# Expert slots of an attention and mixture-of-experts block: hidden transposes behind half of the next up projection, copies in halves, weight splits behind the gating

## What is computed

```
x = x + tanh(g_xattn) * xattn(layernorm(x), ctx)        # 16 heads of 64
xf = layernorm(layernorm(x)) * gamma + beta             # 2048 x 256
probs = softmax(xf @ router_w.T)                        # 8 experts
gate = the two largest probabilities of each token
for each expert e:
    xe = xf * gate[:, e]
    g, u = split(xe @ gate_up_w[e].T)                   # 512 and 512 wide
    out += (silu(g) * u) @ down_w[e].T                  # back to 256
x = x + tanh(g_ffn) * (x' + out)                        # x' is the normed input of this part
```

## Time and profile before

| | us |
|---|---|
| median of three runs (544.29 to 546.94) | 546.45 |
| the profiled execution | 547.43 |
| its span, first to last instruction | 545.1 |
| TensorE busy in the span | 511.6 |
| VectorE busy | 340.2 |
| ACT busy | 290.6 |
| POOL busy | 213.3 |

### The profile page before, as it was taken

The page is one execution under the profiler, slowest core; times in us unless marked ns, Lnnn a source line. Parts: engine busy times, 40 slices in busy tenths (PEclk is TensorE's granted clock), DMA queues, the critical chain, the costliest instruction groups (busy, mean ns, idle before and its releaser), DMA issues.

```text
span 545.1 us, 11962 instructions
## 1 busy us (share of the span) xinstructions
PE 511.6 (94%) x3712; PEld 475.5 (87%) x3712; DVE 340.2 (62%) x811; ACT 290.6 (53%) x881; POOL 213.3 (39%) x242
## 2 busy tenths in 40 slices
PE   7899999999999999999999798989889999999992
PEld 6698999999999999999998687877778888888881
DVE  5956676667768778587685777578745563333330
ACT  3446666656555556456655565576346654444341
POOL 5063100305604569318374168335423343332332
PEclk9999999999999999999998989999999999999997
DMA  8700000499991011100023066554386653343421
GB/s 232 239 0 2 1 1 2 140 304 297 288 290 62 0 39 38 39 0 10 31 78 99 0 207 190 123 134 116 79 240 167 138 78 46 54 60 58 59 30 20
DMA packets 50418, 54.35 MB, mean 100 GB/s; under 512 B 8832, under 2 KB 46464, under 8 KB 50368
## 3 DMA queue, kind: packets, MB, share of 16 engines
q1 hardware_dynamic: 43216, 44.38, 28.5%
q0 software_dynamic: 7152, 9.33, 10.8%
HBM read 24.12 MB, written 29.58 MB: 99 GB/s over the span
## 4 chain that ended last, share of the span: by engine, by line
PE 67%; DVE 12%; issue 6%; DMA 4%; ACT 3%; DVEq 2%; POOLq 2%; POOL 2%; SPq 1%; ACTq 0%
PE bank L914 13%; PE bank L739 9%; PE bank L685 8%; PE bank L763 8%; PE bank L701 8%; PE bank L934 6%; PE bank L715 5%; DMA out_dram<-yq,tok 2%; PE bank L748 2%; PE bank L924 2%; PE bank L859 2%; PE bank L659 1%; DVE nmax L1213 1%; PE bank L782 1%; DVEq L1171 1%
## 5 line engine op out<-in xcount | busy, mean ns | idle before, releaser
L1022 ACT ACTIVATE probs<-bank,nmax 128x154 f32<-128x154 f32 x256 | 98.3, 395 | 81.6 <-DVE nmax L1213 81.6
L602 POOL DMA_INDIRECT out_dram<-yq,tok x39 | 60.8, 1560 | 119.2 <-ACT yq L1101 57.9
L739 PE MATMUL bank<-vdiag,pT 128*128 128x128 f32 (+2 forms) x640 | 79.8, 272 | 1.0 <-DVE oT_lo L1237 0.6
L739 PEld LDWEIGHTS bank<-vdiag,pT 128*128 128x128 f32 (+1 forms) x640 | 77.6, 194 | 1.7 <-DVE oT_lo L1237 1.1
L1213 DVE TENSOR_REDUCE nmax<-bank 128x2 f32<-128x308 f32 x128 | 57.0, 476 | 34.1 <-PE bank L701 33.9
L914 PE MATMUL bank<-gu_hi,xqT_hi 128*128 (+1 forms) x156 | 67.9, 435 | 0.0
L914 PE MATMUL bank<-gu_lo,xqT_hi 128*128 (+1 forms) x156 | 61.5, 394 | 0.0
L914 PE MATMUL bank<-gu_hi,xqT_lo 128*128 (+1 forms) x156 | 61.3, 393 | 0.0
L1580 DVE TENSOR_TENSOR hidT_lo<-bank,hidT_hi 128x512 fp32r<-128x512 f32 x39 | 26.9, 690 | 47.0 <-ACT hidT_hi L1094 46.7
L1575 DVE TENSOR_TENSOR hid<-hid,bank 128x512 f32<-128x512 f32 x39 | 26.8, 687 | 43.1 <-PE bank L914 42.9
L1022 ACT ACTIVATION_READ_ACCUMULATOR probs<-bank,nmax 128x1 f32 x256 | 53.2, 208 | 0.0
(11 more groups left out here) (211 smaller groups left out, 1323.6 us busy)
## 6 DMA issues: line engine op xcount, KB each, us to landing
expert_queue<-zrow SPq DMA_DIRECT2D x8, 2184.5 KB, 23.0
gu_raw<-in_gate_up_wT_dram SPq DMA_DIRECT2D x16, 512.0 KB, 4.3
xq<-expert_queue SPq DMA_DIRECT2D x39, 128.0 KB, 2.9
dn_raw<-in_down_wT_dram SPq DMA_DIRECT2D x8, 512.0 KB, 4.3
x<-in_x_dram SPq DMA_DIRECT2D x4, 512.0 KB, 13.2
out_dram<-out SPq DMA_DIRECT2D x8, 256.0 KB, 4.6
wq_raw<-in_L_xattn_Wq_dram SPq DMA_DIRECT2D x1, 1024.0 KB, 11.7
wo_raw<-in_L_xattn_Wo_dram SPq DMA_DIRECT2D x1, 1024.0 KB, 10.4
```

The source lines that it names most:

```text
L602: nc.gpsimd.indirect_dma_start(out[:, :], bass.IndirectOffsetOnAxis(tok[j % (2 * RT)][:, 0:1], 0), yq[p][:, :], None, compute_op=ALU.add). ...
L739: last = nc.tensor.matmul(at[:, col0 + j0 * DH:col0 + j0 * DH + n], pT[u % 2][0:rows, b, :], v, start=(b == 0), stop=(b == NBLK - 1), skip ...
L1022: last = nc.scalar.activation(probs[u % 4][:, j * NKB:(j + 1) * NKB], S_BANK[hf][:, m * NKB:(m + 1) * NKB], ACT.Exp, bias=nmax[:, u % 4, j ...
```

## The change

The diff is given whole, without blank lines. On TensorE the hidden transposes of tile j-1 go behind the first up half of tile j, so that they stand next to the row transposes of tile j+1. They write two banks: the first two chunks HT_BANK, the last two the bank in which tile j-2's result lay (hidden_bank; TA for the first and the last tile), and so a wait on e_ysb, that this result was read, stands between them. ACT and VectorE copy the hidden rows in two halves, and down waits for each half apart. On VectorE rows_T comes ahead of gated, and the splits that LOWS names come behind gated; two splits, in EARLY_LOWS, stay ahead of both.

```diff
@@ -100,8 +100,9 @@
     HIGHS = {2: ((2, 0), (2, 1)), 3: ((2, 2),), 4: ((3, 0), (3, 1)), 5: ((3, 2),), 6: ((4, 0),), 7: ((4, 1),), 8: ((4, 2),),
              12: ((5, 0),), 13: ((5, 1),), 14: ((5, 2),), 15: ((6, 0),), 16: ((6, 1),), 17: ((6, 2),), 18: ((7, 0),), 19: ((7, 1),), 20: ((7, 2),)}
-    LOWS = {3: ((2, 0),), 4: ((2, 1), (2, 2)), 5: ((3, 0),), 6: ((3, 1),), 7: ((3, 2), (4, 0)), 8: ((4, 1),), 9: ((4, 2),),
-            13: ((5, 0),), 14: ((5, 1),), 15: ((5, 2),), 16: ((6, 0),), 17: ((6, 1),), 18: ((6, 2),), 19: ((7, 0),), 20: ((7, 1),), 21: ((7, 2),)}
+    LOWS = {2: ((2, 0),), 3: ((2, 1),), 4: ((3, 0),), 5: ((3, 1),), 6: ((4, 0),), 7: ((4, 1),), 8: ((4, 2),),
+            12: ((5, 0),), 13: ((5, 1),), 14: ((5, 2),), 15: ((6, 0),), 16: ((6, 1),), 17: ((6, 2),), 18: ((7, 0),), 19: ((7, 1),), 20: ((7, 2),)}
+    EARLY_LOWS = {4: ((2, 2),), 6: ((3, 2),)}
     ON_POOL = ((0, 2), (1, 0), (1, 1), (1, 2))
     with ExitStack() as ctx:
@@ -160,6 +161,10 @@
             hidT_lo = fsb("hidT_lo", [P, KF, P], F32R)
             yq = [fsb(f"yq{n}", [P, D]) for n in range(RT)]
         G_BANK, U_BANK, XT_BANK, HT_BANK, Y_BANK = bank[0], bank[1], bank[6], bank[4], (bank[5], bank[7])
+
+        def hidden_bank(j, h):
+
+            return HT_BANK if h == 0 else TA if j in (0, MT - 1) else Y_BANK[(j + 1) % 2]
         def expert_at(sp, rank):
@@ -919,17 +924,21 @@
                 def transpose_hidden(i, p):
                     j = RT * i + p
                     pe.wait_ge(s["e_hid"], j + 1)
-                    at_least(pe, s["e_hT_lo"], j)
+                    at_least(pe, s["e_hT_lo"], 2 * j)
                     for c in range(KF):
-                        last = nc.tensor.transpose(HT_BANK[:, c * P:(c + 1) * P], hid[:, c * P:(c + 1) * P], ident[:, :])
+                        if c == 2 and 0 < j < MT - 1:
+                            at_least(pe, s["e_ysb"], j)
+                        last = nc.tensor.transpose(hidden_bank(j, c // 2)[:, c % 2 * P:(c % 2 + 1) * P],
+                                                   hid[:, c * P:(c + 1) * P], ident[:, :])
                     last.then_inc(s["e_hT_ps"], 1)
                 def down(i, p, rank):
                     j = RT * i + p
-                    pe.wait_ge(s["e_hT_lo"], j + 1)
                     at_least(pe, s["e_ysb"], j - 1)
                     n = 0
                     for c in range(KF):
+                        if c % 2 == 0:
+                            pe.wait_ge(s["e_hT_lo"], 2 * j + c // 2 + 1)
                         for h, part in ((hidT_hi, dn_hi), (hidT_lo, dn_hi), (hidT_hi, dn_lo)):
                             last = nc.tensor.matmul(Y_BANK[p % 2][:, 0:D], h[:, c, :], weights(part, rank, c * D, D),
                                                     start=(n == 0), stop=(n == 3 * KF - 1))
@@ -947,12 +956,10 @@
                         pe.wait_ge(s["table"], 1)
                     rank = rank_of(i, p)
                     tile_before = (i - 1, RT - 1) if p == 0 else (i, p - 1)
+                    up(i, p, rank, 0, G_BANK, "e_gate", "e_silu")
+                    if j in (2, 3):
+                        turn_features(NI, j - 2)
                     transpose_hidden(*tile_before)
-                    if j == 3:
-                        turn_features(NI, 1)
-                    up(i, p, rank, 0, G_BANK, "e_gate", "e_silu")
-                    if j == 2:
-                        turn_features(NI, 0)
                     if j == 3:
                         router_logits(NI, 0, TA)
                         router_logits(NI, 1, TA)
@@ -1091,7 +1098,10 @@
                     j = RT * i + p
                     act.wait_ge(s["e_hT_ps"], j + 1)
                     at_least(act, s["e_y"], j)
-                    nc.scalar.copy(hidT_hi[:, :, :].rearrange("p c t -> p (c t)"), HT_BANK[:, :]).then_inc(s["e_hT_hi"], 1)
+                    for h in range(2):
+                        part = slice(2 * h, 2 * h + 2)
+                        nc.scalar.copy(hidT_hi[:, part, :].rearrange("p c t -> p (c t)"),
+                                       hidden_bank(j, h)[:, 0:2 * P]).then_inc(s["e_hT_hi"], 1)
                 def scaled(i, p):
@@ -1576,14 +1586,16 @@
                 def hidden_T(i, p):
                     j = RT * i + p
-                    dve.wait_ge(s["e_hT_hi"], j + 1)
-                    nc.vector.tensor_tensor(hidT_lo[:, :, :].rearrange("p c t -> p (c t)"), HT_BANK[:, :],
-                                            hidT_hi[:, :, :].rearrange("p c t -> p (c t)").bitcast(F32), ALU.subtract).then_inc(s["e_hT_lo"], 1)
+                    for h in range(2):
+                        part = slice(2 * h, 2 * h + 2)
+                        dve.wait_ge(s["e_hT_hi"], 2 * j + h + 1)
+                        nc.vector.tensor_tensor(hidT_lo[:, part, :].rearrange("p c t -> p (c t)"), hidden_bank(j, h)[:, 0:2 * P],
+                                                hidT_hi[:, part, :].rearrange("p c t -> p (c t)").bitcast(F32), ALU.subtract).then_inc(s["e_hT_lo"], 1)
                 def expert_slot(i, p, more=True):
                     j = RT * i + p
                     hidden_T(*((i - 1, RT - 1) if p == 0 else (i, p - 1)))
-                    for part in LOWS.get(j, ()):
+                    for part in EARLY_LOWS.get(j, ()):
                         split_low(dve, *part)
                     if j == 2:
                         second_norm(1)
@@ -1593,9 +1605,11 @@
                     if j == COUNT_SLOT:
                         count_rows(NI)
                         number_rows(NI)
-                    gated(i, p)
                     if more:
                         rows_T(i + (p + 1) // RT, (p + 1) % RT)
+                    gated(i, p)
+                    for part in LOWS.get(j, ()):
+                        split_low(dve, *part)
                     if j == COUNT_SLOT - 2:
                         router_probs(NI)
                         choose(NI, 0)
```

## The result

The changed kernel took 552.01 us (median of 7 runs, 550.02 to 553.21) against 546.94 for the kernel before (7 runs, 544.29 to 548.08). The ratio is 1.0107, with a 95% interval of 1.0086 to 1.0128: 4.7 to 7.0 us slower, about 5.9; the two medians differ by 5.1. The profiled execution took 552.01 us, span 549.3. The forecast was 549.0 with a range of 544.0 to 554.5: slower, as the larger chance said, and inside the range, but about 3 us short, and outside the forecast's own range (547.5 to 550.3).

A forecast was written before the change was run, and what follows sets the result against it. TensorE's own work was taken to bound the steady slots (0 us), late VectorE to hold the early ones; routing terms summed to +2.53, say +2.55, on 547.43, less 0.98 to the median: 549.0 us, range 544.0 to 554.5.

The forecast's parts named there:

- Steady slots, 26 x 0: The 26 late expert slots, bound by TensorE's own work at 4.86 us each: nothing saved or lost, 0 us.
- TensorE's queue: Look-up before the up half: margin 0.04 to 0.14 us; rival without that margin, +1.3 to +7.3 us, chance 0.23.
- T: Start of a slot's hidden transposes; down was due at T + 2.04, the next up half at T + 3.48.
- Transposes next to each other: Steady slots: six transposes standing together cost 0.11 us each as before, so nothing is saved.
- (a): Slot 3: the logits wait 1.1 us for the copy of xfT where they waited 0.37, +0.75 us.
- (b): Slot 4: the new wait for e_ysb inside the transposes, with ACT's yq late, delays the hidden copy, +0.45 us.
- (c): VectorE, tile 3 to tile 8: halves +0.30, gaps that do not close +0.75, first half releasing down -0.27 us.
- (d): After each late down the expert look-up is bare, 0.28 us with an up half behind it: +0.15 us.
- (e): Slot 12: the output starts later as slot 10's gating is behind its rows, and tile rows queue behind it: +0.40 us.
- (f): Early splits in slots 4 and 6, counted in (c); tail: last scatter-add waits for the one before, 0 us.
- The clock: Rival: slot 9's wait passes 2 us and the granted clock falls, +1.7 to +3.4 us, 550.7 to 552.4, chance 0.07.
- Faster: Rival: splits behind the gating close VectorE's gaps and slot 3's waits go, 543.3 us, chance 0.13.

The follow-up runs named there:

- before_pool: The kernel before with two weight splits, (3, 0) and (3, 2), made by POOL instead of VectorE: 547.88 us, ratio 1.0050.
- lookup_ahead: The kernel after with the look-up of the next tile's expert moved in front of the second up half: 550.06 us, ratio 1.0071.
- lookup_twice: The kernel after with the expert look-up before the first up half made twice for tiles 14 to 38: 567.85 us, ratio 1.0402.
- whole_copies: The kernel after with hidden copies whole and from one bank for tiles 13 to 38: 566.52 us, ratio 1.0363.
- tile3_whole: The kernel after with tile 3 transposed into one bank and copied whole, without the wait for yq: 552.57 us in one profile.
- splits_alone: The kernel before with only the new split tables and their place behind the gating and the rows: 548.24 us, ratio 1.0044.
- features_first: The kernel after with ACT's copy of xfT in slot 3 moved ahead of the hidden copies: 551.26 us, ratio 1.0077.
- all_edits: The kernel after with look-up moved ahead, xfT copied first, tile 3 whole and two splits on POOL: 550.25 us, ratio 1.0089.

## Why the prediction was right in the sign and short in the size

**Steady slots, 26 x 0: the step that failed.** Three margins were named, and the thinnest, TensorE's queue with 0.04 to 0.14 us, was not there. The first half of the hidden copies was released at T + 1.46 as worked out (T = 483.57; VectorE's pair begins at 484.61 and one half takes 0.42: 485.03). The up half's first weights were due at T + 3.37 (0.12 after 486.82) and forecast for T + 3.34; they loaded at T + 3.45 (487.02). The chain had been put together from a measured 1.78 us and an estimated 0.1 for a second wait; it was 0.1 longer, and 0.1 a slot is 2.5 us. That is the mean: down was released at T + 1.46 in every steady slot, but from tile 12 to 22 a slot lost 0.14 and later 0.07; what makes the queue slower in the earlier ones was not told apart. The mechanism stood among the rivals at 1.3 to 7.3 us, with chance 0.23: its lower part is what happened. Its reason was the wrong one, though. It was tied to long loads (649 ns), but here the look-up is as short as before:

```profile
L905 PEldq TENSOR_LOAD <-table x55: 283/287/422, 400.6 to 535.7; - x55
```

The reason given against that rival held: 2 of these 55 loads took over 320 ns, where before 17 of 54 did. That the long ones come only with an SP issue beside them was a little too strong: in the trace of before 15 of the 17 have one.

The figure of about 600 ns (the Trainium skill, "DMA: Bandwidth & Descriptors", section "Latency and other measured facts") would have given 555.0 by the prediction's estimate; the trace disagrees on the load (287 ns), and the time came out at 552.0. The chain fails already with a short load, because everything between release and next up half goes through one queue. A margin that is a small difference of large terms should not have been booked as zero.

**Transposes next to each other: nothing.** Right: with the look-up moved, the slot is 4.89 us.

**(a) Slot 3, +0.75.** The wait for xfT came, 0.92 us after 0.37, a little under the 1.1 forecast, and tile 2's down stands 0.61 behind; taking the cause away gave back 1.1 us. Right.

**(b) Slot 4, +0.45.** The wait for yq came (0.32), and from tile 2 to tile 3 the change lost 0.61. Removing it gave 0.34 to 0.57. Right.

**(c) VectorE, +0.78.** From tile 3 to tile 8 the loss was 1.06. VectorE waited 0.56 and 0.89 us for rows in slots 4 and 7 (forecast 0.6 and 1.0) and 0.66 and 0.61 for hidden copies behind slots 5 and 6 (0.6 and 0.4), 2.72 in all, where 2.7 was forecast:

```profile
357.73 0.42 DVE L1578 TENSOR_TENSOR xqT_lo<-bank,xqT_hi 128x256 fp32r<-128x256 f32 x1 [0.56 <-ACT xqT_hi L1089]
367.96 0.76 DVE L1592 TENSOR_TENSOR hidT_lo<-bank,hidT_hi 128x256 fp32r<-128x256 f32 x2 [0.66 <-ACT hidT_hi L1103]
374.12 0.76 DVE L1592 TENSOR_TENSOR hidT_lo<-bank,hidT_hi 128x256 fp32r<-128x256 f32 x2 [0.61 <-ACT hidT_hi L1103]
375.77 0.42 DVE L1578 TENSOR_TENSOR xqT_lo<-bank,xqT_hi 128x256 fp32r<-128x256 f32 x1 [0.89 <-ACT xqT_hi L1089]
```

So the gaps grew as forecast, +0.77 against +0.75. The stretch between the hidden copies grew by 1.41, because VectorE's busy time grew by more than the +0.30 too, from 25.84 to 26.48; down after a first half alone gave back 0.35 of it (forecast 0.27). The picture of VectorE's work plus gaps fits the trace of after; no run took the work away to test it, since before_pool did not.

**(d), (e), +0.55 together.** Tile 8 to tile 12: +0.39. (d) booked 0.15 with 0.28 for one late up half. Behind each of the four downs that were waited for (363.71, 381.14, 388.59 and 399.70) the next up half's first two matmuls lost 0.28, 0.38, 0.46 and 0.29 us against their usual distances, 1.4 in all (before lost 0.1 to 0.2 behind tiles 4, 8 and 10). What that cost in time is open: lookup_ahead has none of these four, but it waits 1.4 us for its queue in front of second up halves in their place. For (e), the rows of tile 13 come at 403.99 in after, 1.4 later than in the earlier trace rows and 2.4 from the common origin, with the wait for their DMA down from 1.18 to 0.48, so part of the delay is absorbed there.

**(f) The tail, 0.** Right. The last scatter-add still waits for the one before it:

```profile
541.57 1.54 POOL L607 DMA_INDIRECT out_dram<-yq,tok  x1 [2.94 <-DMA out_dram<-yq,tok]
```

**The clock, a rival with 0.07.** Under-rated. In after's first profile it stayed at 1.00, in the second it fell, so 2.67 + 2.50 = 5.2 us without a fall and 6.5 with one frame the measured 5.9. lookup_twice and whole_copies run the same instructions as after up to slot 12; the clock fell in both, and their tile 12 stands 4.13 and 3.75 behind. So three of four profiles of these slots had a fall, and the agreement of 2.67 with the 2.55 is that of the one without. The place was right only in part (slot 9 in some profiles, slot 3 in others). A fall costs about 1.0 to 1.1 us at the next down, less than the 1.7 forecast; of one in slot 9 between 0.1 (lookup_twice) and 1.3 (tile3_whole) is left at tile 12.

**Faster, a rival with 0.13.** It needed VectorE's gaps to close when the splits go behind the gating. splits_alone does just that on the old order, and is slower.

Of the list of what would show it: waits for xfT, for yq and for rows were there; down of tile 8 is 2.28 us later from the common origin, 1.21 by the span's own clock ("about 2"); steady slots longer than 4.90 were named as the sign of the queue, and 4.964 was that sign.

## What to carry to other kernels

When a step is moved next to a late release, count the whole way from the release through the engine's instruction queue to the next group's first weight load, with every register look-up on it, and do not book a margin of 0.1 us as safe: here it was 0.1 us of loss in every slot. A TensorE that the profile shows as fully busy can still lose 2% a slot: compare the distance between starts at the borders of groups, not the busy share. And when work is moved to another engine, read in the trace how long the steps that run beside it now take: here two splits moved to POOL gave VectorE back 0.2 us of their 2.4.

## What the runs showed of the hardware

Behind a wait of TensorE its granted clock may fall to 0.50 for some 3 us, or may not, in executions of the same program. In features_first, before and in such a fall:

```profile
385.40:387.80 2.40, 0.46 (x3) 0.04 (x1) 2.02 (x9) 0.43 (x2) 2.10 (x2) 1.00 0.25 87
388.60:391.80 3.20, 3.20 (x13) 2.81 (x12) 0.23 (x1) 0.47 (x1) 0.66 (x1) 0.50 0.71 123
```

And in after at the same place, without one:

```profile
385.40:388.60 3.20, 1.24 (x7) 0.69 (x5) 2.67 (x12) 1.19 (x4) 2.59 (x3) 1.00 0.23 82
389.00:392.00 3.00, 2.80 (x18) 2.29 (x17) 0.60 (x2) 0.48 (x1) 0.14 (x1) 1.00 0.61 98
```

After 330 us there was a fall in 8 of the 10 profiles with the new order of the transposes and in 2 of 4 with the old one, none in the two of before itself. The mean clock of each timed run points the same way: its median is 0.981 to 0.985 for eight of the nine edited versions that were timed, 0.984 for after, and 0.987 to 0.989 for the runs of before beside them (before_pool 0.982 against 0.989). A fall of some 3 us at half clock takes about 0.003 of such a mean (an estimate from the 545 us of a run), so one or two falls more a run would do it. That the edited kernels fall more often fits, but the means don't say where in the span the clock fell, and what decides between the two outcomes stays open.

A VectorE step beside a long POOL step may be held until that ends: 1.53, 0.97 and 2.21 us where 0.17 to 0.19 is usual, beside splits of 2.4 us in before_pool and all_edits. In before_pool the gating (0.68 us from 361.49) and the rows (0.42 from 362.08) ran beside the same split at their usual length; which steps are held is not told by these runs.
